# Four-column-tile layer norm statistics, a one-matmul spread of the reciprocal deviation, and a projection split over two 64-column tiles

## The reference, cut to what matters

```python
x = conv_block_0(x); x = conv_block_1(x)          # routed 1x1 -> 3x3 depthwise -> 1x1, 24 -> 96 -> 24
x = x + attention(layernorm(x))                   # 6 heads, over the 3136 positions
x = x + ffn_0(layernorm(x))                       # 24 -> 96 -> 24, fp8 products, fp16 sums
x = x + fourier(layernorm(x))                     # 1x1 to 48, FFT over positions, complex mix, relu, inverse FFT, 1x1 to 24
x = x + ffn_1(layernorm(x))

def _layernorm(x, axis=-1, eps=1e-05):
    m = jnp.mean(x, axis=axis, keepdims=True)
    v = jnp.var(x, axis=axis, keepdims=True)
    return (x - m) / jnp.sqrt(v + eps)
```

## Time and profile before

| | us |
|---|---|
| median of 3 runs | 2803.33 (2799.18 to 2808.28) |
| the profiled execution | 2798.5 |
| its span, first to last instruction | 2796.5 |

### The profile page before, as it was taken

One profiled execution on the slowest core, in us unless ns is written; L12 is line 12 of the kernel. 1 busy time (PEld: TensorE's weight loads), 2 busy tenths in 40 slices (PEclk: granted clock), 3 DMA queues, 4 the chain that ended last, 5 costly groups with the idle time before them and its releaser, 6 DMA issues.

```text
span 2796.5 us, 46610 instructions
## 1 busy us (share of the span) xinstructions
PE 2463.6 (88%) x18624; PEld 1413.1 (51%) x18624; DVE 1950.9 (70%) x3622; ACT 1682.0 (60%) x2834; POOL 70.6 (3%) x123
## 2 busy tenths in 40 slices
PE   3867988999979998999989998999989998987776
PEld 1323433666436744664436644466436744673562
DVE  4765877785957887797866786876857888355243
ACT  2334445765667577765666567665667667657534
POOL 1000000000000000000000000000000000000000
PEclk9977989998989999999969998999979999787865
DMA  4001000100020001000010001000010000000000
GB/s 133 1 1 18 1 1 1 19 1 1 1 35 2 2 1 29 8 1 1 10 26 2 1 1 31 5 2 1 1 25 2 1 1 18 1 1 4 15 1 18
DMA packets 108582, 29.63 MB, mean 11 GB/s; under 512 B 104144, under 2 KB 104272, under 8 KB 107984
## 3 DMA queue, kind: packets, MB, share of 16 engines
q1 hardware_dynamic: 108368, 26.65, 4.7%
HBM read 17.00 MB, written 9.63 MB: 10 GB/s over the span
## 4 chain that ended last, share of the span: by engine, by line
PE 66%; DVE 15%; ACT 14%; issue 4%; SPq 1%; DMA 0%; ACTq 0%; DVEq 0%
PE P L664 12%; PE P L645 10%; PE P L709 7%; PE P L679 6%; PE P L857 4%; PE P L700 4%; DVE acc L1348 4%; PE P L898 4%; PE P L685 3%; PE P L870 3%; ACT H L1016 2%; PE P L882 2%; PE P L810 2%; DVE SQ L1483 1%; PE P L725 1%
## 5 line engine op out<-in xcount | busy, mean ns | idle before, releaser
L1348 DVE SCALAR_TENSOR_TENSOR acc<-H,Dm,acc 128x784 f32<-128x784 f32 x1024 | 991.6, 1026 | 119.9 <-ACT acc L1024 119.5
L645 PE MATMUL P<-T,Wk 96*128 96x448 f32 (+1 forms) x768 | 409.9, 618 | 68.5 <-ACT H L1016 46.5
L664 PE MATMUL P<-H,diag 64*64 64x392 f32 x4608 | 403.9, 500 | 1.5 <-ACT H L1016 0.8
L1016 ACT ACTIVATE H<-P,biasA 128x448 f32<-128x448 f32 (+1 forms) x384 | 238.6, 621 | 258.9 <-PE P L645 209.4
L664 PEld LDWEIGHTS P<-H,diag 64*64 64x64 f32 x4608 | 172.0, 135 | 214.8 <-issue 207.2
L709 PE MATMUL P<-T,pack_b 96*96 96x448 f32 x448 | 245.0, 638 | 34.1 <-DVE T L1444 19.0
L645 PEld LDWEIGHTS P<-T,Wk 96*128 96x128 f32 x768 | 132.5, 207 | 216.1 <-ACT H L1016 122.0
L679 PE MATMUL P<-acc,Wk 128*96 128x392 f32 x512 | 200.2, 538 | 14.6 <-ACT acc L1053 14.5
L1047 ACT ACTIVATE acc<-P,biasT 128x392 f32<-128x392 f32 x128 | 68.4, 584 | 204.1 <-PE P L664 204.0
L882 PE MATMUL P<-pack_b,arena 128*96 128x112 f32 x928 | 118.4, 280 | 30.7 <-DVE arena L1483 17.3
L679 PEld LDWEIGHTS P<-acc,Wk 128*96 128x96 f32 x512 | 87.3, 178 | 111.8 <-issue 111.2
(11 more groups left out here) (198 smaller groups left out, 4156.8 us busy)
## 6 DMA issues: line engine op xcount, KB each, us to landing
xin<-in_x SPq DMA_DIRECT2D x224, 42.0 KB, 2.2
out_y<-arena SPq DMA_DIRECT2D x8, 1176.0 KB, 5.7
pack_b<-in_pack_b SPq DMA_DIRECT2D x1, 3820.0 KB, 17.9
arena<-in_pack_s SPq DMA_DIRECT2D x1, 1780.0 KB, 9.0
pack_a<-in_pack_a SPq DMA_DIRECT2D x1, 1084.0 KB, 5.2
pack_i<-in_pack_i SPq DMA_DIRECT2D x1, 318.0 KB, 2.9
arena<-in_pack_k SPq DMA_DIRECT2D x1, 192.0 KB, 3.1
```

Of the source, the lines that this page charges most:

```text
L645: pe.matmul(conv_rows(slice(0, 128), H1B, m), Wk1[:, 128 * (u % NT):128 * (u % NT + 1)], image_rows(T[q % 3], a + r0, m), start=True, stop ...
L664: last = pe.matmul(conv_rows(slice(64 * h, 64 * (h + 1)), CVB + r, HH), diag[64 * r:64 * (r + 1), tap, :], H1[64 * r:64 * (r + 1), slot(s, ...
L1016: act.activation(H1[:, slot(s, j), o + r0:o + r0 + m, 1:1 + HW], conv_rows(slice(0, 128), H1B, m), ACT.Relu, bias=biasA[:, j, 1:2]).then_i ...
L1348: ins = ve.scalar_tensor_tensor(a, H1[:, slot(s, j), r:r + SR, c:c + HW], Dm[:, j, tap:tap + 1], a, ALU.mult, ALU.add)
```

## The change

**Layer norms.** A chunk is now four blocks of 112 positions (`LT` = 4, `LN_N` = 112). `variance(c)` issues four fp32 matmuls of 112 columns with 32-column weights, into PSUM partitions 0, 32, 64 and 96, so the statistics of a quad are a tile of 128 partitions x 112 columns. ACT's root and DVE's reciprocal and split run on 112 columns. The three bf16 terms are copied by twelve small DVE copies (32 partitions x 112) into one tile `thirds` of 96 partitions x 448 columns, and a chunk is spread with one bf16 matmul of 448 columns.

**The projection.** `UV[:, 2k+j, :]` is taken as two weights, of 64 and 56 columns, which go to PSUM partitions 0 to 63 and 64 to 119; each runs against `fw2` once, 48 columns. Five frequencies make a group instead of four (6 groups instead of 8), the copies of ACT and the weights of the second inverse step have 120 partitions, and `g` has rows of zeros for the eight partitions between.

**The order.** The four strings of `TURNS` are written anew: PE's has 2520 steps instead of 2536 and ACT's 2265 instead of 2281 (two projection groups fewer in each of 8 quads), DVE's has 2073 and POOL's 103, as before. PE's first 65 steps are the same; after that the interleaving differs throughout.

```diff
-LB = 14
-LN_N = TOK // LB
+LT = 4
+LN_N = CK // LT
+KR = 64 + HW
...
                 def variance(c):
                     pe.wait_ge(norm.sq_ready.sem, norm.sq_ready.at(q, N0 + c + 1))
-                    o = (LB // 2 - 1 - c) * QI
-                    for t in range(2):
-                        sq = LN_N * ((2 * c + t) % 4)
-                        last = pe.matmul(P[64 * t:64 * (t + 1), norm.var, 0:LN_N], par["selv"][0:R, o:o + 64],
+                    o = (NCK - 1 - c) * QI
+                    for t in range(LT):
+                        sq = CK * (c % 2) + LN_N * t
+                        last = pe.matmul(P[32 * t:32 * (t + 1), norm.var, 0:LN_N], par["selv"][0:R, o:o + 32],
                                          norm.SQ[:, sq:sq + LN_N], start=(c == 0), stop=(c == NCK - 1))
...
-                    for h in range(2):
-                        dst = P[0:R, norm.spread[c % NSP], LN_N * h:LN_N * (h + 1)]
-                        pe.matmul(dst, selb16[:, 2 * c + h, :], norm.rb2, start=True, stop=False)
-                        last = pe.matmul(dst, selb16[:, 2 * c + h, :], norm.rb3, start=False, stop=True)
-                    last.then_inc(norm.rs_psum.sem, 1)
+                    pe.matmul(P[0:R, norm.spread[c % NSP], 0:CK], selb16[0:96, c, :], norm.thirds[:, :, :].rearrange("p t n -> p (t n)"),
+                              start=True, stop=True).then_inc(norm.rs_psum.sem, 1)
...
-            KG, KP = 4, 120
+            KG = 5
...
-                            o = KP * (k % KG) + 2 * CH * j
-                            last = pe.matmul(P[0:2 * HW, B0 + g % BN, o:o + 4 * CH].rearrange("p (a n) -> p a n", a=2), UV[:, 2 * k + j, :],
-                                             twice, start=True, stop=True)
+                            o = R * (k % KG) + 2 * CH * j
+                            for p, a, n in ((0, 0, 64), (64, HW, HW)):
+                                last = pe.matmul(P[p:p + n, B0 + g % BN, o:o + 2 * CH], UV[:, 2 * k + j, a:a + n],
+                                                 par["fw2"][0:R, :], start=True, stop=True)
...
-                rest, third = norm.sdev, norm.rstd
-                link(ve.tensor_copy(norm.rb2, norm.rstd), q, half)
-                link(ve.tensor_tensor(rest, norm.rstd, norm.rb2, ALU.subtract), q, half)
-                link(ve.tensor_copy(norm.rmid, rest), q, half)
-                for h in range(2):
-                    ve.tensor_copy(norm.rb2[64 * h + 32:64 * h + 60, :], norm.rmid[64 * h:64 * h + 28, :])
-                link(ve.tensor_tensor(third, rest, norm.rmid, ALU.subtract), q, half)
-                ve.tensor_copy(norm.rb3[0:32, :], third[0:32, :])
-                ve.tensor_copy(norm.rb3[64:96, :], third[64:96, :]).then_inc(norm.rs_ready.sem, 1)
+                rest, (high, middle_, low) = norm.sdev, norm.terms
+                link(ve.tensor_copy(high, norm.rstd), q, half)
+                link(ve.tensor_tensor(rest, norm.rstd, high, ALU.subtract), q, half)
+                link(ve.tensor_copy(middle_, rest), q, half)
+                link(ve.tensor_tensor(low, rest, middle_, ALU.subtract), q, half)
+                for k, term in enumerate(norm.terms):
+                    for t in range(LT):
+                        last = ve.tensor_copy(norm.thirds[32 * k:32 * (k + 1), t, :], term[32 * t:32 * (t + 1), :])
+                last.then_inc(norm.rs_ready.sem, 1)
```

More of the change, by code:

```diff
@@ L65 @@
              ("wr", (E,)), ("br", (16,)), ("wkx", (HID + 1, E)), ("wd", (NT, DCOL, E)))],
-    "s": [("selb", (LB, R)), ("fbn1", (4, 2 * R)), ("fbn2f", (2, 2 * CH))]
+    "s": [("selb", (NCK, R)), ("fbn1", (4, 2 * R)), ("fbn2f", (2, 2 * CH))]
          + [(f"{n}{L}", s) for L in range(2) for n, s in (
              ("w1", (NT * 128,)), ("b1", (NT,)), ("w2", (NT, R)), ("b2", (1,)))],
-    "b": [("cen", (R,)), ("selv", (64 + (LB // 2 - 1) * QI,)), ("m97", (R + 1,)),
+    "b": [("cen", (R,)), ("selv", (32 + (NCK - 1) * QI,)), ("m97", (R + 1,)),
           ("s97", (R,)), ("wva", (CH,)), ("wkbd", (R,)), ("bk", (1,)), ("wqt", (CH + 1,)),
@@ L80 @@
 TURNS = {
+    "gpsimd": (
+        "d7 b1 c10 m1 c10 m1 c6 b1 c4 m1 c6 b1 c4 m1 c6 b1 c4 m1 c6 b1 c4 m1 c6 b1 c4 m1 c6 b1 c4 m1 b1 "
+    ),
     "tensor": (
[43 rows of a table removed]
[45 rows of a table added]
     ),
@@ L127 @@
         "c4 m1 c13 d2 c1 d1 c2 d1 c5 d2 c1 d1 c2 d1 c5 d2 c1 d1 c2 d1 c4 d4 c10 d2 c1 d1 c2 d1 c4 m1 c1 d2 c1 "
[36 rows of a table removed]
[37 rows of a table added]
     ),
     "vector": (
[25 rows of a table removed]
-    ),
-    "gpsimd": (
-        "d7 b1 c11 m1 c11 m1 c8 b1 c2 m1 c7 b1 c3 m1 c8 b1 c4 m1 c6 b1 c5 m1 c5 b1 c2 m1 c7 b1 c1 m1 b1 "
[22 rows of a table added]
     ),
@@ L214, in __init__, with small @@
         self.n, self.D, self.SQ, self.cen, self.var, self.spread = n, D, SQ, cen, var, spread
+    def small(self, room, thirds):
+        self.sdev, self.rstd = room[:, 0:LN_N], room[:, LN_N:2 * LN_N]
+        terms = room[:, 2 * LN_N:2 * LN_N + 3 * LN_N // 2].bitcast(BF16)
+        self.terms = [terms[:, LN_N * k:LN_N * (k + 1)] for k in range(3)]
+        self.thirds = thirds
 class Ffn:
@@ L280, in build @@
         qb8 = sb("qb8", [128, 2, NT + 1], F8)
-        selb16 = sb("selb16", [128, LB, R], BF16)
+        selb16 = sb("selb16", [128, NCK, R], BF16)
         eps = sb("eps", [128, 2])
@@ L316, in build @@
         normM = Norm(n=0, D=Yf, SQ=z[0:R, 0:2 * CK], cen=(3,), var=4, spread=(3, 4))
-        z2 = z[:, 2 * CK:2 * CK + 3 * LN_N]
-        normM.sdev, normM.rstd = z2[:, 0:LN_N], z2[:, LN_N:2 * LN_N]
-        normM.rmid = z2[:, 2 * LN_N:2 * LN_N + LN_N // 2].bitcast(BF16)
-        normM.rb2, normM.rb3 = (sb(name, [128, LN_N], BF16)[:, :] for name in ("rb2m", "rb3m"))
+        normM.small(z[:, 2 * CK:], sb("thirdsm", [96, LT, LN_N], BF16))
         YT = z[0:BLK, 0:2 * BPG * (R + 1)].rearrange("p (b n) -> p b n", b=2 * BPG)
@@ L330, in build @@
         normB = Norm(n=2, D=Y, SQ=SQ[0:R, :], cen=(5, 6), var=7, spread=(5, 6, 7))
-        roots = sb("roots", [128, 2 * LN_N])
-        normB.sdev, normB.rstd = roots[:, 0:LN_N], roots[:, LN_N:]
-        normB.rmid = SQ[:, 0:LN_N // 2].bitcast(BF16)
-        normB.rb2, normB.rb3 = (sb(name, [128, LN_N], BF16)[:, :] for name in ("rb2b", "rb3b"))
+        roots = sb("roots", [128, CK])
+        normB.small(roots, sb("thirdsb", [96, LT, LN_N], BF16))
         T = Ts
@@ L355, in build @@
         Y2 = arena[:, reg1:reg1 + K1 * 2 * R].rearrange("p (k j c) -> p k j c", k=K1, j=2)
-        S2 = arena[0:2 * HW, reg1:reg1 + K1 * R].rearrange("p (k n) -> p k n", k=K1)
+        S2 = arena[0:KR, reg1:reg1 + K1 * R].rearrange("p (k n) -> p k n", k=K1)
         Wf = arena[0:R, reg1 + K1 * R:reg1 + reg2].rearrange("p (x k) -> p x k", x=HW)
@@ L450, in build @@
         ffns[1].banks, ffns[1].out_bank = (5, 6), 7
-        NX, NA, NW, NBI, NTR, NFO = 14, 12, 8, 8, 6, 7
+        NX, NA, NW, NBI, NTR, NFO = 14, 12, 6, 8, 6, 7
         NSG = -(-2 * K1 // 4)
-        KG, KP = 4, 120
+        KG = 5
         fpads_set = sig("fourier_pads_set", 3)
@@ L554, in _ @@
             for n, (dst, value) in enumerate((
-                    (eps[:, 0:1], 1e-5), (eps[:, 1:2], 1e-3), (H1[:, :, :, :].rearrange("p a r w -> p (a r w)"), 0.0),
-                    (normM.rb2, 0.0), (normM.rb3, 0.0), (normB.rb2, 0.0), (normB.rb3, 0.0))):
+                    (eps[:, 0:1], 1e-5), (eps[:, 1:2], 1e-3), (H1[:, :, :, :].rearrange("p a r w -> p (a r w)"), 0.0))):
                 pool_e.memset(dst, value).then_inc(consts_set.sem, 1)
@@ L835, in middle @@
                     pe.wait_ge(par_loaded["b"].sem, 16)
-                    pe.wait_ge(consts_set.sem, 7)
+                    pe.wait_ge(consts_set.sem, 3)
                     pe.wait_ge(setup_late.sem, 1)
@@ L884, in fourier @@
                     last.then_inc(sp_psum.sem, 1)
-                twice = par["fw2"][0:R, :].unsqueeze(1).broadcast_to([R, 2, 2 * CH])
                 for g in range(NW):
@@ L911, in fourier @@
                         o = 2 * HW * (k % 4)
-                        last = pe.matmul(P[0:R, B0 + g % BN, o:o + 2 * HW], S2[:, k, :], par["g"][0:2 * HW, k, :],
+                        last = pe.matmul(P[0:R, B0 + g % BN, o:o + 2 * HW], S2[:, k, :], par["g"][0:KR, k, :],
                                          start=True, stop=True)
@@ L1168, in fourier @@
                     act.activation(S2[:, KG * g:KG * g + n, :],
-                                   P[0:2 * HW, B0 + g % BN, 0:KG * KP].rearrange("p (s n) -> p s n", s=KG)[:, 0:n, 0:R],
+                                   P[0:KR, B0 + g % BN, 0:n * R].rearrange("p (s n) -> p s n", s=n),
                                    ACT.Copy).then_inc(s2_ready.sem, 1)
@@ L1539, in _shape_constants @@
     c["cen"] = np.eye(R) - same / CH
-    selv = np.zeros((R, 64 + (LB // 2 - 1) * QI))
-    selv[np.arange(R), (LB // 2 - 1) * QI + row_i] = 1.0 / CH
-    selb = np.zeros((128, LB, R))
-    for b in range(LB):
-        p = 64 * (b % 2) + b // 2 * QI + row_i
```

(11 more changed lines are left out.)

## The result

The changed kernel takes 2732.03 us (median of 4 runs, 2728.32 to 2732.27) against 2801.73 us (2799.18 to 2808.28) for the kernel before, measured beside it: a ratio of 0.973, 95% interval 0.9701 to 0.9759, 70 us faster. The profiled execution has a span of 2730.1 us. The forecast was 2735 us.

A forecast was written before the change was run, and what follows sets the result against it. PE was taken to bound the kernel, 94% busy in the middle. Of 110 us of chain (spread 35, variances 33, projection 42) 83 arrive, less 2 for small steps and 13 for clock: -68 us, 2735 us, range 2680 to 2797.

The forecast's parts named there:

- L897's records: Projection on PE: 232 smaller records a quad, 29 ns apart at full clock, -42 us on the chain.
- Spread 0.19 and 0.37: Norms' spread on PE: one 448-column matmul a chunk, 0.19 us at full clock, 0.37 at half; -35 us on the chain.
- Variance 0.38 and 0.57: Norms' variance on PE: us a chunk to the next matmul at full and half clock; -33 us on the chain.
- my lower bound: Variance chunk on PE: 0.34 us if pure streaming decides, -40 us on the chain.
- DVE's split 3.6 to 4.4: Norm on DVE, reciprocal to last copy: 3.6 to 4.4 us, no change within 0.5 from 4.05.
- Rival (1): Small tiles cost by the record, 60 ns apart: slower, about 2828 us, 8%; for the projection alone 2786 us, 6%.
- My estimate by that page: Projection on PE by the skill's overhead: 200 ns for one weight without overlap, no gain; 100 ns if tiles overlap.
- the sum: Whole kernel: 110 us of chain cut by a quarter to -83, then +2 and +13, giving -68 us.
- the products' pace: DVE's products after the spread take 0.61 us or more a chunk, so without other PE work it gains 0.1, not 0.37.
- The clock step: Last quad's L857 and L870: clock may not rise after the thinned spread, up to 25 us more; half booked, +13.
- rival (2): Clock stays at half in both last quads' first Fourier steps: +50 instead of +13, 2772 us, 14%.
- The order was booked at nothing, +-20 us: New order of steps throughout the kernel: no price in the trace, so 0 us booked, left at +-20 us.

The follow-up runs named there:

- e6: The changed kernel with the variance's moving operand given twice, 224 columns in each of the four tiles: 2765.18 us.
- e3: The changed kernel with the old projection put back (112-column weights), new order and new layer norms kept: 2762.88 us.
- e4: The changed kernel with the old layer norms (variance, split and spread), new projection and new order kept: 2748.45 us.
- e2: The kernel before with the new order of steps, two projection steps a quad added: 2779.40 us, ratio 0.992 to the kernel before.
- e10: The changed kernel with each spread matmul issued twice and the variance's moving operand given twice: 2766.29 us.
- e1: The changed kernel with the old order of steps, less two projection steps a quad: 2777.89 us, ratio 0.991 to the kernel before.
- e5: The changed kernel with each spread matmul issued twice, same operands into the same place: 2752.02 us.

## Why the prediction was right, and where it was not

**Right in its whole.** 2735 us were forecast and 2732 measured. That PE is what bounds the middle, that small column tiles overlap, and that the lines touched hold some 290 us of the chain, held.

**The durations held.** L897's records, forecast at 29 ns: 29 from start to start at full clock, 53 at half against 58. Spread 0.19 and 0.37: (1.32 - 0.58) / 2 = 0.37 at half. Variance 0.38 and 0.57: 0.33 and 0.53, so eight records are not held to 29 ns each and streaming decides, as in my lower bound and as e6 shows. DVE's split 3.6 to 4.4: 4.34. The products I took at 0.61 us or more each; in the last norm they come at 0.54. Rival (1), records 48 ns apart or more, is ruled out.

The Trainium skill ("TensorEngine Tiling (Array Packing)", Instruction Overhead) advises against taking a tiling factor from a dimension that is already small. My estimate by that page was 200 ns for one weight without overlap and 100 with it; the four records of one weight take 117 ns in the changed kernel's trace, so this case agrees with the overlap, and by e3 the split brings 31 us.

**The step "the sum" was wrong in how it gets there.** I took a quarter off 110 us of the chain, alike for all parts. The projection lost that quarter (31 of 42). The norms lost three quarters (16 of 68). The cause that I named, the products' pace and waits uncovered on DVE, is the small part: PE's waits grew by 9.5 us from e4 to the changed kernel. What the runs show in its place is the granted clock, down 0.03 by the new norms (e2 to e3, e4 to changed), and by the spread above all (e10 to e6). The norms gave PE 80 us, more than the 68 of my chain, and 52 of them went back into other matmuls that now ran at half clock.

**The clock step named the right thing and the wrong place.** I booked 13 us for the last quad's L857 and L870, with rival (2) for two quads. There it cost little: the clock rose 6.4 us into L856 and that stage took 16.0 us instead of 14.5. It was lost instead throughout the run, most of it behind the thinned spreads, where I had looked for nothing, though I had written that a fall by 0.03 would break the forecast. From old to new norms it did fall by 0.03; against the kernel before by 0.016, since the new order alone raised it from 0.896 to 0.905.

**The order was booked at nothing, +-20 us.** It is worth 25 us with the old code (e2), and 46 with the new (e1 to changed). Without it the change would have stood at 2778, inside my range but 43 us off. The nearly exact hit is thus errors that cancel. The norms were booked at 51 us (three quarters of 68) and gave 16, 35 too much; the 13 us booked for the clock are within what e4 against the changed kernel measures of the norms, so the code as a whole was booked 20 us too high (68 less 47), and the order 22 to 25 too low.

**Open.** Why the clock is lower behind a thin spread is not shown, only that a second matmul of the same operands keeps it higher (e10 against e6, e5 against the changed kernel). Nor is it shown why the order moves the clock. The sum of the norms' parts isn't settled either: doubling the variance's columns costs 33 us with the spread thin, and an amount not known within some 15 us with it doubled, since the runs of e5 and e10 scatter by over 20 us.

## What to carry to other kernels

Price the removed work by start-to-start distances, and expect it to arrive only as far as the other engines and the order of steps follow: cross the old and new code with the old and new order before crediting either. Work taken from TensorE can be paid back by a lower granted clock: compare the time of the matmuls that the change doesn't touch, and the clock by stretches, not only the total. On an engine that isn't the bound, eight small copies cost a third of their time here, not nothing. And look in the trace whether an edit did save what it was meant to save, before its time is taken for an answer.

## What the runs showed of the hardware

Four tiles of 32 weight columns and 112 moving fp32 columns do run beside each other: eight records and what lies around them take 0.33 us, against 0.53 for two tiles of 64 and 224, and 0.52 for four tiles with 224 (e6). So about 0.14 us a chunk does not depend on the columns. Two tiles with 48 moving columns come at 29 ns a record at full clock. Single-tile fp32 records with 96 weight columns stay 85 ns apart even with one moving column. I had not expected that 43 us of repeated spread matmuls could be free: 2765 us without them, at a mean granted clock of 0.877 to 0.881, and 2766 with them, at 0.894 to 0.906.
